# Reordered stack loads in the head and new orders for four filling iterations of a pipelined transformer block

## The reference

```
x = attention(ln1(x), ln1(x), Wq1, Wkv1, Wo1, bo1) + x
x = attention(ln2(x), context, Wq2, Wkv2, Wo2, bo2) + x
x = geglu_ff(ln3(x), Wff1, bff1, Wff2, bff2) + x
```

## Time and profile before

| | us |
|---|---|
| median of the runs | 1665.45 |
| profiled execution, its own time | 1666.33 |
| its span, first to last instruction | 1664.5 |
| TensorE busy (matmul) | 1564.9 (94%) |
| VectorE busy | 1102.0 (66%) |
| ScalarE busy | 995.7 (60%) |
| GpSimd busy | 253.2 (15%) |

### The profile page before, as it was taken

One profiled execution on the slowest core, in us unless ns is written; L12 is line 12 of the kernel. 1 busy time (PEld: TensorE's weight loads), 2 busy tenths in 40 slices (PEclk: granted clock), 3 DMA queues, 4 the chain that ended last, 5 costly groups with the idle time before them and its releaser, 6 DMA issues.

```text
span 1664.5 us, 33969 instructions
## 1 busy us (share of the span) xinstructions
PE 1564.9 (94%) x12833; PEld 1008.8 (61%) x12833; DVE 1102.0 (66%) x2269; ACT 995.7 (60%) x2024; POOL 253.2 (15%) x342
## 2 busy tenths in 40 slices
PE   6888999999999999999999999999999999998887
PEld 5544445476766757576666657565665656564766
DVE  4556677767768685867768685867768675843433
ACT  4344666675766666675756666665656656674442
POOL 1210321111202111111202111101101001101110
PEclk9999999999999999999999999999999989998999
DMA  8812241427231241537131241355121231303210
GB/s 236 200 46 90 92 77 53 110 69 141 51 83 56 63 100 53 109 74 146 51 73 50 71 85 52 77 95 111 46 58 49 54 59 46 81 26 82 55 34 13
DMA packets 177116, 129.76 MB, mean 78 GB/s; under 512 B 40975, under 2 KB 168889, under 8 KB 176697
## 3 DMA queue, kind: packets, MB, share of 16 engines
q1 hardware_dynamic: 176889, 127.58, 32.3%
q10 hardware_dynamic: 64, 0.02, 0.0%
HBM read 79.24 MB, written 47.71 MB: 76 GB/s over the span
## 4 chain that ended last, share of the span: by engine, by line
PE 68%; DVE 17%; DMA 6%; ACT 3%; SPq 3%; issue 2%; POOL 0%; DVEq 0%; ACTq 0%; POOLq 0%
PE ps_o L1708 10%; PE ps_last L1621 10%; PE ps_max L1678 10%; PE ps_s L1696 9%; DVE mxh L1359 8%; PE ps_last L1630 6%; PE ps_pre L1485 4%; DVE mx L1285 4%; PE ps_cross L1589 3%; PE ps_pre L1493 3%; PE ps_cross L1575 3%; DMA o_s<-den_c 2%; DMA den_c<-o_s 1%; PE ps_last L1643 1%; PE ps_last L1658 1%
## 5 line engine op out<-in xcount | busy, mean ns | idle before, releaser
L1359 DVE TENSOR_REDUCE mxh<-ps_max 128x1 f32<-128x512 f32 x1024 | 656.1, 682 | 206.2 <-PE ps_max L1678 204.5
L1142 ACT ACTIVATE probs<-ps_s 128x512 f32<-128x512 f32 x1024 | 580.7, 597 | 245.6 <-PE ps_s L1696 193.4
L1678 PE MATMUL ps_max<-kst,qst 96*128 96x512 bf16 x1024 | 373.2, 388 | 32.7 <-DVE mxh L1359 16.3
L1696 PE MATMUL ps_s<-qst,kst 98*128 98x256 bf16 x2048 | 369.1, 275 | 8.6 <-ACT probs L1142 6.5
L1696 PEld LDWEIGHTS ps_s<-qst,kst 98*128 98x128 bf16 x2048 | 177.7, 98 | 155.0 <-ACT probs L1142 53.6
L1708 PE MATMUL ps_o<-probs,vg 128*17 128x256 f32 x4096 | 269.3, 385 | 0.0
L1678 PEld LDWEIGHTS ps_max<-kst,qst 96*128 96x128 bf16 x1024 | 96.0, 97 | 157.3 <-DVE mxh L1359 90.7
L1086 ACT ACTIVATE probs<-ps_cross 77x512 f32<-77x512 f32 x224 | 132.7, 592 | 78.8 <-PE ps_cross L1575 77.9
L1317 DVE SCALAR_TENSOR_TENSOR th<-th,gb 128x256 f32<-128x256 f32 x128 | 56.9, 444 | 163.9 <-ACT gb L1117 163.9
L1708 PEld LDWEIGHTS ps_o<-probs,vg 128*17 128x17 f32 x4096 | 96.7, 97 | 112.0 <-issue 52.3
L1621 PE MATMUL ps_last<-y_hi,wff_hi 128*128 128x256 f32 x448 | 139.6, 312 | 4.2 <-DVE y_lo L1311 2.5
(11 more groups left out here) (261 smaller groups left out, 1947.1 us busy)
## 6 DMA issues: line engine op xcount, KB each, us to landing
parts_s<-qk_parts SPq DMA_DIRECT2D x28, 384.0 KB, 4.3
o_s<-o_sb SPq DMA_DIRECT2D x64, 128.0 KB, 2.5
o_s<-o_sb SPq DMA_DIRECT2D x32, 256.0 KB, 2.2
oT<-o_s SPq DMA_DIRECT2D x62, 128.0 KB
den<-o_s SPq DMA_DIRECT2D x62, 128.0 KB
q_s<-qk_parts SPq DMA_DIRECT2D x16, 384.0 KB, 2.3
q2st<-q_s SPq DMA_DIRECT2D x16, 384.0 KB, 5.4
q2st<-q_s SPq DMA_DIRECT2D x48, 128.0 KB, 6.1
```

The lines of the kernel that those rows point to most:

```text
L1142: nc.scalar.activation(probs[:, step % PR, 2 * pair:2 * pair + 2, :].rearrange("p j q -> p (j q)"), ps_s[pair][:, :], ACT.Exp, scale=SCALE ...
L1359: nc.vector.tensor_reduce(mxh[:, i % PAIRS, i // PAIRS:i // PAIRS + 1], ps_max[i % 2][:, :], AX_X, ALU.max).then_inc(g_mx, 1)
L1678: mm(ps_max[i % 2][:, :], qst[0:ROWS, h, q * P:(q + 1) * P], kst[0:ROWS, h, half * 512:(half + 1) * 512], start=True, stop=True).then_inc( ...
L1696: last = mm(ps_s[pair][:, j * CH:(j + 1) * CH], kst[:, h, kt * P:(kt + 1) * P], qst[:, h, :], start=True, stop=True)
```

## The change

Two edits; no instruction is added or taken away.

In the head, the load of chunk 2's key stack for heads 8 to 15 moves from the loop (iteration p = 3) to behind the load of chunk 3's stack for heads 0 to 7. So chunk 3's values store and its stack for the first head groups are issued four transfers sooner.

The four filling strings are written anew. Over all four each letter occurs as often as before, but the borders between the strings lie elsewhere: FIRST now has 29 `M` in place of 18, and 18 setup steps in place of 15; SECOND begins with 13 tiles of unit 1 already issued. In FIRST, eight setup steps and three steps of *pre* stand before the first `M`; before, it was one setup step. The projections of *pre* 4, which stood together behind the first `T`, are spread among the maxima. In FOURTH, `m` steps 1 to 3 come later, the last `m` (the store of q2) comes after `d`, and `x` after `i`.

```diff
 FIRST = (
-    "sMssspspMMsMspsMMsMMpMsMssMMsMsMMsMQTpppMpM"
+    "sspsssssppsMsMpMMsMsMMpMssMMMMMsMMMpQTMMsMMMMpMpMMsMMsMMs"
 )
 SECOND = (
-    "MMSMMSMSMMSMSMSMsMSMSVMSMQSTSMMSSVMSsMSMMSSVMMSSssMpOSpMSMVMMSVM"
-    "SMSpsVMQTSpMSMSMuSMSMsSpMSMpSMVSMSVMMspMSMOMMMpQsSSTuMVSMMSMSMoS"
-    "SMsSMsVMSMSSMVMSSMsSoMSMVOuMMSQTMMSMSsVMoSSMMSMSsMSSMSMSSMVSMSsM"
-    "SMOMSVMQTVSMSMM"
+    "MMSpSMSQSTSSMMVSMSMVSMSMSMSMSspSMSVSMMpSsMMSSVMOSpMSSMQVSSTVSMM"
+    "sMSSMpMMSSuVSMoSMpSMMVSMoMOpMSMSMSMQusTSSVSMSMSMSMVSMoSMspMMSsMM"
+    "sSSMMVOSMSMVMMQsSSTsSMMSVMSMSMSSMMVMMSSMSMSMSMSMVuMSsMSQVTuO"
 )
 THIRD = (
-    "SSSMsMSSMMMMVSSMMuSSMMosVMmSpSMmMsSQSVTSSMpMSVOSMuSVSoSmMpMVuSMp"
-    "MSSMsMpMMSSMpMMSVMMSSpQTVOspSmMSMMSSsMMMSSsMSmMSMVVMSMSmSMSMSMSM"
-    "SmMQVToSsuSMMmMSMmVSMMOSSMSMSVSSoMMVMSSMMSMSSMMSQSOx"
+    "SSsMMSSMoSMVMSMSSMMVMSMSMuSMSMSMSMSMVpQSmTSVpMOSSMMpSVMSMmSpMSMV"
+    "MsSSMpMMSSMpMMSSmVSMuMQpToSVmMOpSoMSMSMSMSMSMSmSsMVMSSVsmMMSSMSo"
+    "MSMmSMSMVSQsTmMMVMsOSMSMSMSMVMSMSMSMSSmMMSSMVMusMQxSS"
 )
 FOURTH = (
-    "VTSVSMMMSMSMMcVSMcMSMcSSMSSMcScSoMMmVSSccMSMSMucmSpQcSVuTcScMSpM"
-    "cSVMOSScpVSoSMMcScVMMpcMSMpMmSMcMuMScMpScVSMMScpcQTVcSmOcpuoMScM"
-    "SMcSScMMSSMMcSmScVMSMcMmSSMVMcSMSMmMcSMQVTScSMcMSmcMMmcSMMcSMVSO"
-    "MSdSVSMSMVMSSMMSSMSMMxQSoifSeVTVO"
+    "sVTSSMMVMsMSMSOcMuSMScMcuSSMcVMScMSVcSMcSMSopMcSMSSMcSQcVSTScVS"
+    "pMSMccOSMSpVSMSMcScpScMSVMSMmpMMcmSMSMcpMcMVMSmSoMcpuQcSTVcmcMSM"
+    "pcSMSMcMSMcSMmSOMcSMVcmSMSoMcVSMSMcSMmMcSMQSVuTScSMScMSOVcSMMScm"
+    "MMcMdSSMVmMSMSMVMSMSMSeSMixMSSQoVfTVO"
 )
...
                     elif p:
                         head_stack(p - 1, (1,), 0)
-                        head_stack(p - 1, (1,), 1)
+                        if p == 2:
+                            head_stack(1, (1,), 1)
...
                 head_stack(MAX_LAG - 1, (1,), 0)
+                head_stack(MAX_LAG - 2, (1,), 1)
                 head_stack(0, (0,), 1)
                 head_stack(MAX_LAG - 1, (1,), 1)
```

More of the change, by code:

```diff
@@ L64 @@
 FIRST = (
-    "sMssspspMMsMspsMMsMMpMsMssMMsMsMMsMQTpppMpM"
+    "sspsssssppsMsMpMMsMsMMpMssMMMMMsMMMpQTMMsMMMMpMpMMsMMsMMs"
 )
 SECOND = (
-    "MMSMMSMSMMSMSMSMsMSMSVMSMQSTSMMSSVMSsMSMMSSVMMSSssMpOSpMSMVMMSVM"
-    "SMSpsVMQTSpMSMSMuSMSMsSpMSMpSMVSMSVMMspMSMOMMMpQsSSTuMVSMMSMSMoS"
-    "SMsSMsVMSMSSMVMSSMsSoMSMVOuMMSQTMMSMSsVMoSSMMSMSsMSSMSMSSMVSMSsM"
-    "SMOMSVMQTVSMSMM"
+    "MMSpSMSQSTSSMMSVSMSMVSMSMSMSMSspSMSVSMMpSsMMSSVMOSpMSSMQVSSTVSMM"
+    "sMSSMpMMSSuVSMoSMpSMMVSMoMOpMSMSMSMQusTSSVSMSMSMSMVSMoSMspMMSsMM"
+    "sSSMMVOSMSMVMMQsSSTsSMMSVMSMSMSSMMVMMSSMSMSMSMSMVuMSsMSQVTuO"
 )
 THIRD = (
-    "SSSMsMSSMMMMVSSMMuSSMMosVMmSpSMmMsSQSVTSSMpMSVOSMuSVSoSmMpMVuSMp"
-    "MSSMsMpMMSSMpMMSVMMSSpQTVOspSmMSMMSSsMMMSSsMSmMSMVVMSMSmSMSMSMSM"
-    "SmMQVToSsuSMMmMSMmVSMMOSSMSMSVSSoMMVMSSMMSMSSMMSQSOx"
+    "SSsMMSSMoSMVMSMSSMMVMSMSMuSMSMSMSMSMVpQSmTSVpMOSSMMpSVMSMmSpMSMV"
+    "MsSSMpMMSSMpMMSSmVSMuMQpToSVmMOpSoMSMSMSMSMSMSmSsMVMSSVsmMMSSMSo"
+    "MSMmSMSMVSQsTmMMVMsOSMSMSMSMVMSMSMSMSSmMMSSMVMusMQxSS"
 )
 FOURTH = (
-    "VTSVSMMMSMSMMcVSMcMSMcSSMSSMcScSoMMmVSSccMSMSMucmSpQcSVuTcScMSpM"
-    "cSVMOSScpVSoSMMcScVMMpcMSMpMmSMcMuMScMpScVSMMScpcQTVcSmOcpuoMScM"
-    "SMcSScMMSSMMcSmScVMSMcMmSSMVMcSMSMmMcSMQVTScSMcMSmcMMmcSMMcSMVSO"
-    "MSdSVSMSMVMSSMMSSMSMMxQSoifSeVTVO"
+    "sVTSSMMVMsSMSMSOcMuSMScMcuSSMcVMScMSVcSMcSMSopMcSMSSMcSQcVSTScVS"
+    "pMSMccOSMSpVSMSMcScpScMSVMSMmpMMcmSMSMcpMcMVMSmSoMcpuQcSTVcmcMSM"
+    "pcSMSMcMSMcSMmSOMcSMVcmSMSoMcVSMSMcSMmMcSMQSVuTScSMScMSOVcSMMScm"
+    "MMcMdSSMVmMSMSMVMSMSMSeSMixMSSQoVfTVO"
 )
```

## The result

The changed kernel takes **1641.97 us** (median of 1640.21 and 1643.74), before 1665.45: a ratio of 0.9856, 95% interval 0.9836 to 0.9876. The direction was right and the size was half of what came. The change stays within 2%, as forecast at 0.97. What happened is what the rival "the small waits go too" described, with its 1640 to 1646 us and its chance of 0.11.

The account below looks back on a forecast made before the run. TensorE was taken as the bound, with 33.85 us open in the fill. Gains of 8.0 and 4.0 less a cost of 0.5 gave 11.5 off 1666.33: 1654.8, or 1654 on the median's footing; range 1642 to 1664.

Parts of the forecast that it names:

- the small waits go too: Rival: TensorE in the fill gets as dense as later, 31 us less; half likelier, given as 1640 to 1646; chance 0.11.
- part 3: SECOND to FOURTH, from unit 1's transpose on: finer order removes small waits, gain 4.0 us, ends 0 and 12.
- Part 2: The gap before unit 0 up to unit 1's transpose: setup steps fill it, gain 8.0 us, ends 5 and 11.
- The clock that I left open: Ahead of unit 0: at the low clock, setup steps 6 to 8 would last twice as long, some 1.5 us more.
- The rule cited from the Trainium skill: Matmuls want to run back to back; small spaced steps ahead of unit 0 would not lift the clock: 7.5, not 9.0.
- part 1: The head's loads: one group of four moves behind another; gain taken as 0, cost at most 0.9 us if uncovered.
- The first *cross* tile still waits for its stack: Sign of being right: the 1.88 us wait, 22.4 us after q2's projection, stays, so no gain is booked there.
- The q2 store behind `d`: Iteration 7, SyncE: q2's store now stands behind the wait of `d`; cost 0.5 us taken, between 0 and 3.3.
- The waits ahead of the transposes: Sign of being right: fewer than 2.5 us of waits ahead of the 13 transposes in the fill, 4.9 before.
- a second stretch at a low clock: Sign of being wrong: another stretch where TensorE's granted clock is low; no size given.
- Kept only in part: Rival: other engines and the q2 chain set the fill after unit 1; lead shrinks to 2 to 5 us, 1661 to 1664; chance 0.16.
- Unit 0 held by VectorE's order: Rival: first maximum slips 4.5 us and everything ends later, 1670, if its distance to the transpose stays over 17.2; chance 0.08.

Follow-up runs that it names:

- e3: The kernel before with the new head loads and new SECOND to FOURTH but old FIRST, the missing `M` and `s` put ahead of SECOND: 1647.38 us, 0.9891.
- e2: The kernel before with the new head loads and new FIRST; SECOND to FOURTH old, less what FIRST had already done: 1659.6 us, 0.9965.
- e1: The kernel before with only the head's loads in the new order, all four strings old: 1665.41 us, 1.0005.
- e4: The changed kernel with the four loads of the first *cross* key stack issued earlier, in step 3 of the middle stage: 1637.25 us, 0.9829 of the kernel before.
- e14: The changed kernel with the borders of its units untouched and the 16 `M` of an interval in four runs of four: 1727.1 us, 1.0369 of the kernel before.
- e10_port: e4 with the last weight splits moved in THIRD behind the last step of the middle stage: 1634.17 us, 0.9806 of the kernel before.

## Why the prediction was right and where it failed

**The failing step is the term of part 3**, "Gain 4.0; ends 0 ... and 12", taken "near the low end, as no row says which of the small waits go". It measured some 18 us (e3) by the times, 19.7 by the transposes. Two things were left out. First, I counted waits by the name of what released them and booked only those at the borders; but from unit 1's to unit 6's transpose TensorE's open time went from 11.71 to 1.38, so the waits for maxima and exponents (3.0 and 1.7 us there before) went with them. They are one family: a step that runs ahead of VectorE or ScalarE. Second, I booked no gain for busy time. From unit 1's to unit 13's transpose the old order took 228.7 us, 208.5 of them busy, the new one 209.0, with 200.5 busy at matmul counts of 1634 and 1653. So of 19.7 us won there, 11.7 were open time and 8.0 were time shown as busy. The granted clock (0.97 and 0.98) is some 2.7 of the 8.0, as (1 - 0.97) x 228.7 - (1 - 0.98) x 209.0, an estimate from rounded clocks. The other 5.3 are most likely waiting that the rows show as busy. Two rows of the kernel before:

```profile
125.39 0.39 PE L1678 MATMUL ps_max<-kst,qst 96*128 96x512 bf16 x1 [0.21 <-DVE mxh L1359]
125.99 0.39 PE L1678 MATMUL ps_max<-kst,qst 96*128 96x512 bf16 x1 [0.21 <-DVE mxh L1359]
```

These tiles come every 0.60 us, VectorE's pace, and 0.21 of it is shown as idle. But a tile holds the next instruction up for only 0.22 (215.43 to 215.65 above), so 0.38 was lost and 0.17 of that is counted as busy, at each wait behind a tile. From unit 1's to unit 13's transpose there were 43 waits before and 7 after; 36 x 0.17 = 6.1, an estimate, which with the 2.7 makes up the 8.0 within the rounding. So even the idle time in the earlier trace rows was too small a measure of what waits cost, and the upper end of 12 was too low.

What spoke for the high end was in the rows: the full pipeline runs the same tiles and scores, mixed with other steps, with 0.8 us open in 90, so "TensorE in the fill as dense as later" was within reach. The rival's figures are not what its text says, though: half of its 31 us is 1650, and 1640 to 1646 is 19 to 25 of the 31. Its mechanism was right; that its range held the time owes something to that slip.

**Part 2** was too large: 8.0 forecast, 5.4 at unit 1's transpose. The some 6 of e2 are no second proof, as they were won later. The path was right, the times were not. The wait ahead of unit 0 shrank to 2.90 (3 forecast), but the first tile came at 46.71 in place of 44, the first maximum at 48.76 in place of 46.9, and unit 0's transpose at 64.14 in place of 61.5, level with before. From the first tile to the transpose it took 17.4 us, 17.5 forecast: what was lost was lost ahead of the tile. The next 14.5 us (13 to 14 forecast) carry the whole gain; unit 1's transpose, at 78.63, is 3.6 behind the forecast 75. The clock that I left open was the lower one, 0.70 and 0.73 in the two stretches where the new small steps stand; it came up once TensorE was busy throughout, in the second of them. The rule cited from the Trainium skill, Perfetto Trace Analysis, section Matmul Optimizations, has these rows for it: steps spaced by copies, 2.63 us busy in 6.00, ran at the lower clock in part (0.70), so the trace agrees that far. The sum by it, 7.5, was still above 5.4. Two readings were off by little: the normalisation's 1.29 in the earlier trace rows was itself drawn out (last section; 0.74 after), and ahead of unit 1's transpose stand two setup steps more, not one, and four score tiles behind unit 0's, not five.

**Right**: part 1 at 0 (e1, with the old strings). The first *cross* tile still waits for its stack, 22.4 us behind q2's projection in both kernels (197.05 to 219.48 after), so the chain of copies, stores and loads kept its length; issuing four of its loads earlier took the wait away (e4). The q2 store behind `d` at 0.5 (0.77 measured, 0 to 3.3 given). The waits ahead of the transposes at under 2.5 (0.2). The stretch of 7.67 on VectorE without a maximum is gone. One sign of being wrong came too, a second stretch at a low clock (0.69 from 220 to 230); the kernel before had it as well, at 240.

**The rivals.** "Kept only in part" is out: the lead of unit 1 grows. "Unit 0 held by VectorE's order" has its first half, as the first maximum slipped 6.4 us, more than the 4.5 assumed; but the distance to the transpose, 64.14 - 48.76 = 15.4, is under its deciding 17.2. The time fell to "the small waits go too".

## What to carry to other kernels

Where one engine issues by a fixed order and feeds two slower ones, lay out that order so that each feed comes at its consumer's pace: alternate the two kinds, put long work between, and leave cover on both sides of every round trip. Repairing one wait of such an order moves it; count the sum of all waits in the stretch, not the ones that carry the name you work on. For a forecast of a fine reorder, take the density that the same engine reaches elsewhere in the same profile as the upper bound of what can go (31 us here, 23.5 came), and a sum of the waits that can be named as a lower one (4.0 for part 3, which gave 18).

## What was not expected of the hardware

**VectorE stood still for GpSimd.** The new wait of 2.21 at 192.88 follows the pair of normalisations at 189.61, 2.62 us in place of 0.74 at 47.72. GpSimd's timeline there in the changed kernel:

```profile
189.54 2.54 POOL L869 TENSOR_TENSOR wff_lo<-hT,wff_hi 128x512 fp32r<-128x512 f32 x2
```

Two subtractions of a weight split end to end, over the same 2.6 us. In e10_port the splits come later. VectorE's and GpSimd's timelines there:

```profile
188.83 0.74 DVE L1238 TENSOR_SCALAR den<-x,mv,rs 128x256 f32<-128x256 f32 x2
```

```profile
189.43 1.27 POOL L879 TENSOR_TENSOR wff_lo<-hT,wff_hi 128x512 fp32r<-128x512 f32 x1 [0.63 <-ACT wff_hi L1041]
```

Off the subtraction, the pair takes 0.74 and the wait is gone. One normalisation takes 1348 ns beside it and 404 to 408 ns otherwise, while reductions out of PSUM go on at their length beside GpSimd in e10_port. It is no single case: in the kernel before, 16 of 96 normalisations are drawn out, to 0.80 us and more, every one beside a GpSimd operation on two tiles; the 65 with nothing on GpSimd beside them take at most 0.42, and 15 beside other GpSimd work or a part of such an operation at most 0.46. The pair of 1.29 at 49.79 in the earlier trace rows is one of them. The Trainium skill, SBUF — State Buffer, section SBUF: two separate sides, says that these two engines share a pair of ports under an exclusive lock, and that, when VectorE's operation is in a mode that uses both its ports, the one that comes second stands still for the other's whole instruction. That the normalisation is in such a mode no run shows; for the rest the trace agrees: each normalisation here is 0.94 us longer, within one subtraction's 1.27, and ends 0.15 us after it.

**A rule that costs 85 us.** Putting the same `M` in runs of four, which also brings together what stood between them, moved the kernel from 1642 to 1727 (e14): the waits for maxima are 18.4 us in 133, and the granted clock fell to 0.90 in that stretch, so part of the loss is the waits and part is the clock behind them.
